# Six-block transformer kernel: a shorter opening, a branch laid the other way round, and new places for the pieces

## The reference

```python
x = x + xattn4(layernorm(x), ctx_1024, itok, ...)      # 4 layers, below, then rmsnorm
x = x + ternary_attention(layernorm(x), u, v)          # qz_u, qz_v, sigmoid, back through u and v
x = x + ffn(layernorm(x), weight, disha)
x = x + perceiver_attention(ctx_1024, layernorm(x), mask, ...)   # 64 latents over 1601+64 keys
x = x + rope_attention(layernorm(x), w_qkv, w_out)
x = x + experts(layernorm(x), ...)                     # 8 experts, the 2 best of a token

def xattn4(x, memory, seg_ids, ...):
    allowed = (j <= seg_ids) & (j > seg_ids - 128)      # j counts the rows of memory, seg_ids per token
    for l in range(4):
        h = rmsnorm(x, n1[l]); q, k, v = split(h @ Wqkv[l].T + bqkv[l])
        x = x + softmax(rope(q) @ rope(k).T * scale + causal) @ v @ Wo[l].T + bo[l]
        h = rmsnorm(x, n2[l]); kc, vc = split(memory @ Wkv_c[l].T)
        x = x + softmax((h @ Wq_c[l].T) @ kc.T * scale + cross_bias(allowed)) @ vc @ Wo_c[l].T
        h = rmsnorm(x, n3[l])
        x = x + silu(h @ Wg[l].T) * (h @ Wu[l].T) @ Wd[l].T
    return rmsnorm(x, nf)
```

## Time and profile before

| | |
|---|---|
| runs before | 500.36 us median, 498.7 to 501.63 |
| profiled execution | 499.64 us, span 497.5 us |
| PE busy | 465.2 us, 94% of the span |
| DVE, ACT, POOL busy | 358.0, 268.5, 227.9 us |
| opening, before the first matmul | 0 to 8.6 us |
| four layers | to about 215 us |
| the five other blocks | about 217 to 495 us |

### The profile page before, as it was taken

One profiled execution on the slowest core, in us unless ns is written; L12 is line 12 of the kernel. 1 busy time (PEld: TensorE's weight loads), 2 busy tenths in 40 slices (PEclk: granted clock), 3 DMA queues, 4 the chain that ended last, 5 costly groups with the idle time before them and its releaser, 6 DMA issues. The chain is left out here.

```text
span 497.5 us, 14297 instructions
## 1 busy us (share of the span) xinstructions
PE 465.2 (94%) x5430; PEld 401.7 (81%) x5430; DVE 358.0 (72%) x1025; ACT 268.5 (54%) x718; POOL 227.9 (46%) x342
## 2 busy tenths in 40 slices
PE   3899999999999999968999998899999998999997
PEld 3667887788778876967999887789999887689997
DVE  4395668566856786656887889999989987654643
ACT  4377757775777577614334475556466554442221
POOL 2871377137613851243799322767889322300000
PEclk9999999999999999979999999999999999999999
DMA  8601020101029000040210432031020000000000
GB/s 252 276 3 32 10 84 2 40 22 65 3 64 381 2 3 1 2 130 17 70 49 24 157 111 67 2 133 60 10 69 3 2 1 1 1 2 1 12 1 12
DMA packets 9953, 27.08 MB, mean 54 GB/s; under 512 B 1346, under 2 KB 4759, under 8 KB 9623
## 3 DMA queue, kind: packets, MB, share of 16 engines
q1 hardware_dynamic: 9878, 26.09, 15.5%
HBM read 25.82 MB, written 0.26 MB: 52 GB/s over the span
## 5 line engine op out<-in xcount | busy, mean ns | idle before, releaser
L913 POOL TENSOR_TENSOR rstd<-ss,par 128x1 f32<-128x1 f32 x52 | 28.5, 549 | 100.8 <-ACT sq L737 100.8
L759 ACT ACTIVATE pr<-sd 128x512 f32<-128x512 f32 x56 | 34.5, 626 | 5.4 <-DVE sd L816 4.9
L1243 POOL TENSOR_TENSOR xh<-xh,rsx 128x512 f32<-128x512 f32 (+1 forms) x32 | 29.8, 931 | 2.5
L1241 POOL TENSOR_TENSOR xh<-cx,mvx 128x512 f32<-128x512 f32 (+1 forms) x32 | 29.4, 918 | 2.7 <-DMA cx<-ctx_in 1.4
L741 ACT ACTIVATE h<-y,rstd 128x128 f32<-128x128 f32 x48 | 19.1, 399 | 9.5 <-POOL rstd L913 9.4
L1222 DVE BATCH_NORM_STATS2 stx<-cx 128x6 f32<-128x128 f32 x104 | 22.7, 276 | 0.5 <-DMA cx<-ctx_in 0.5
L1772 POOL TENSOR_TENSOR rstd<-mv,par 128x1 f32<-128x1 f32 x20 | 4.1, 207 | 39.8 <-DVE mv L1602 36.3
L737 ACT ACTIVATE sq<-y 128x129 f32<-128x129 f32 x52 | 15.9, 306 | 10.0 <-DVE y L847 8.6
L907 POOL TENSOR_TENSOR kblk<-qk,cf 128x512 f32<-128x512 f32 x20 | 20.8, 1040 | 0.9
L1232 POOL TENSOR_TENSOR rsx<-rsx,par 128x13 f32<-128x13 f32 x8 | 20.4, 2546 | 0.6
L1791 POOL TENSOR_SCALAR rk<-kss 128x8 f32<-128x8 f32 (+1 forms) x32 | 7.5, 235 | 24.0 <-DVE kss L1668 22.5
(11 more groups left out here) (570 smaller groups left out, 1507.2 us busy)
## 6 DMA issues: line engine op xcount, KB each, us to landing
cx<-ctx_in SPq DMA_DIRECT2D x13, 768.0 KB
we<-we_in SPq DMA_DIRECT2D x8, 514.0 KB, 7.1
wc<-wc_in SPq DMA_DIRECT2D x4, 768.5 KB, 5.8
wa<-wa_in SPq DMA_DIRECT2D x5, 387.0 KB, 3.0
wb<-wb_in SPq DMA_DIRECT2D x4, 256.5 KB, 3.8
uvT<-uvT_in SPq DMA_DIRECT2D x1, 1024.0 KB, 7.1
uv<-uv_in SPq DMA_DIRECT2D x1, 1024.0 KB, 8.6
cx<-ctx_in SPq DMA_DIRECT2D x13, 32.5 KB
```

The lines of the kernel that those rows point to most:

```text
L759: nc.scalar.activation(pr[:, t, at:at + 512], sd[:, t, at:at + 512], ACT.Exp).then_inc(s[piece], 1)
L913: nc.gpsimd.tensor_tensor(rstd[:, t:t + 1], ss[:, t:t + 1], par[:, 1:2], ALU.pow).then_inc(s[piece], 1)
L1241: step(pool, "pool_step", nc.gpsimd.tensor_tensor(part, cx[u % 2][:, tiles, :], mvx[:, b, tiles, 0].unsqueeze(2).to_broadcast(shape), ALU. ...
L1243: nc.gpsimd.tensor_tensor(part, part, rsx[:, b, tiles].unsqueeze(2).to_broadcast(shape), ALU.mult).then_inc(xm["c_normed"], 1)
```

## The change

1. SP issues `x` first, then one row of token values (`segi`, 1 partition) for the flag, then `cf`, `wa`, `bo`, `memT`, `wb`, `trig`, `cb`, and only then the broadcast `segr`.
2. DVE casts the one row into `pts`; `segf` and `cmask` come at the end of DVE's opening, behind `y`.
3. POOL zeroes `vblk` and `vcblk` at its very start; DVE copies `mem4` behind `y`. ACT's opening keeps only the two relus.
4. `FIRST` gives layer 0's `memory`, `mem_k`, `mem_v` and `kc` own places: no longer in front of everything but one by one between the pieces of the first half of layer 0. PE's queue now begins `turn1.0 project.0 turn1.1 values.0 project.1 memory.0 turn1.2 causal.0 values.1 project.2 scores.0 memory.1`, ACT's `square1.0 norm1.0 hT1.0 square1.1`, POOL's `pow1.0 pow1.1 pow1.2 rope_sum.0`.
5. The general path's semaphores share those of the CROSS pieces, and the 17 counts are made in the general path only.
6. On PE the branch is laid the other way round (`falls="end"`): the test is followed by the general path, and the fast one lies behind it, running straight on into `x_queue`.
7. ACT's and DVE's jump over their general path moves forward: on ACT before the last two `square_f`, on DVE before the last `z_moments`, `norm_f`, `x_f` and the last two `z_norm`. Those pieces are now in `x_queue`.
8. All places are given anew. In the layers this moves `memory`, `cmask`, `cturn`, `cout`, `turn3` and others by a few positions and POOL's `kc` ahead of `pow3`; behind the join some 20 positions differ on PE (`z_turn.2` now before `across0.0`), and POOL's `x_bias` comes later.

```diff
-PERIOD, SKEW = 95.43, (0.0, 6.74, 13.36, 19.85)
+PERIOD, SKEW = 95.05, (0.0, 6.68, 13.36, 19.84)
...
+FIRST = {"memory": 7.91, "mem_k": 8.44, "mem_v": 13.69, "kc": 9.26}
...
 def late(p, l, t):
-    return l * PERIOD + PLACE[p] + SKEW[t]
+    return l * PERIOD + (PLACE[p] if l else FIRST.get(p, PLACE[p])) + SKEW[t]
...
-        self.first = {e: 1 + max(n for n, z in enumerate(q) if z[1] == 0) for e, q in self.queue.items()}
+        self.first = {e: 1 + max(n for n, z in enumerate(q) if z[1] == 0 and not (e == "ACT" and z[2] == LAYERS) and
+                                 not (e == "DVE" and z[2] == LAYERS and z[3:] != (1, "z_norm"))) for e, q in self.queue.items()}
...
         def sp_opening(sp):
-            sp.dma_start(segr[:], seg_in.to_broadcast([P, B * L])).then_inc(s["seg_loaded"], 16)
             sp.dma_start(x[:], x_in.rearrange("(t p) d -> p t d", p=P)).then_inc(s["x_loaded"], 16)
+            sp.dma_start(segi[:], seg_in).then_inc(s["row_loaded"], 16)
+            sp.dma_start(cf[:], cf_in).then_inc(s["cf_loaded"], 16)
+            load_a(sp, 0)
             sp.dma_start(memT[:], memT_in).then_inc(s["mem_loaded"], 16)
             load_b(sp, 0)
-            sp.dma_start(cf[:], cf_in).then_inc(s["cf_loaded"], 16)
-            load_a(sp, 0)
             sp.dma_start(trig[:], trig_in).then_inc(s["trig_loaded"], 16)
             sp.dma_start(cb[:], cb_in).then_inc(s["trig_loaded"], 16)
+            sp.dma_start(segr[:], seg_in.to_broadcast([P, B * L])).then_inc(s["seg_loaded"], 16)
             sp.dma_start(nf[:], nf_in.to_broadcast([P, D])).then_inc(s["trig_loaded"], 16)
...
         def pool_opening(pool):
+            for blocks in (vblk, vcblk):
+                nc.gpsimd.memset(blocks[:], 0.0).then_inc(s["zeroed"], 1)
...
-            act.wait_ge(s["mem_loaded"], 16)
-            nc.scalar.copy(mem4[:], memT[:].unsqueeze(2).to_broadcast([P, B, 4, KF])).then_inc(s["zeroed"], 1)
-            for blocks in (vblk[:].rearrange("p t b j a e -> p (t b j a e)"), vcblk[:].rearrange("p b g i e -> p (b g i e)")):
-                nc.scalar.activation(blocks, par[:, 2:3].to_broadcast([P, B * 4 * 4 * 9]), ACT.Copy, scale=0.0).then_inc(s["zeroed"], 1)
...
-            for name in sorted(set(gsem) - {"ctx_loaded"}):
-                dve.sem_inc(gsem[name], 1)
             nc.vector.memset(y[:, :, D:D + 1], (RMS_EPS * D) ** 0.5).then_inc(s["y_ready"], 1)
-            dve.wait_ge(s["seg_loaded"], 16)
-            nc.vector.tensor_copy(segf[:], segr[:]).then_inc(s["seg_steps"], 1)
+            dve.wait_ge(s["zeroed"], 2)
...             (the ones into vblk and vcblk, moved here)
+            dve.wait_ge(s["row_loaded"], 16)
+            nc.vector.tensor_copy(pts[0:1, 0, 0:B * L], segi[:]).then_inc(s["seg_steps"], 1)
             dve.wait_ge(s["x_loaded"], 16)
...             (behind the four y)
+            dve.wait_ge(s["mem_loaded"], 16)
+            nc.vector.tensor_copy(mem4[:], memT[:].unsqueeze(2).to_broadcast([P, B, 4, KF])).then_inc(s["mem_spread"], 1)
+            dve.wait_ge(s["seg_loaded"], 16)
+            nc.vector.tensor_copy(segf[:], segr[:]).then_inc(s["cmask_set"], 1)
+            dve.wait_ge(s["cmask_set"], 1)
             dve.wait_ge(s["cf_loaded"], 16)
             nc.vector.tensor_scalar(cmask[:], segf[:], jcol, NEG, ALU.is_lt, ALU.mult).then_inc(s["cmask_set"], 1)
...
-        def either(eng, fast, whole):
+        def either(eng, fast, whole, falls="start"):
...
-            with eng.If(few == 1):
-                fast()
+            with eng.If(few == (1 if falls == "start" else 0)):
+                (fast if falls == "start" else whole)()
             with eng.Else():
-                whole()
+                (whole if falls == "start" else fast)()
...
-                either(pe, lambda: opening(pe, x_pe_piece, pe_piece, "PE"), whole)
+                either(pe, lambda: opening(pe, x_pe_piece, pe_piece, "PE"), whole, falls="end")
```

More of the change, by code:

```diff
@@ new lines @@
+    "PE": {"memory": -57.56, "turn1": -5.13, "project": 0.00, "values": 2.34, "causal": 8.35, "scores": 14.14,
+           "turna": 21.06, "turnb": 21.66, "weigha": 23.65, "weighb": 26.52, "turn_o": 27.96, "out": 30.78,
+           "turn2": 37.22, "qc": 38.13, "cmask": 40.25, "cscores": 40.99, "cturn": 48.74, "cweigh": 52.25,
+           "cturn_o": 54.41, "cout": 58.74, "turn3": 65.32, "gate": 67.23, "up": 71.70, "down": 79.16},
+    "ACT": {"square1": -11.89, "norm1": -8.90, "mem_k": -49.93, "hT1": -6.10, "q_groups": 9.94, "expa": 17.65,
+            "expb": 19.69, "turneda": 20.17, "turnedb": 22.51, "oT": 28.78, "square2": 31.68, "norm2": 33.63,
+            "hT2": 35.90, "qcT": 38.41, "cexp": 45.92, "cturned": 49.48, "coT": 54.02, "square3": 58.53,
+            "norm3": 59.59, "hT3": 63.65, "tanh": 67.72},
@@ L75 @@
+    "DVE": {"mem_v": -40.94, "rope": 2.09, "vblk": 7.76, "maxa": 15.75, "maxb": 15.97, "shifta": 16.67,
+            "shiftb": 17.90, "recip": 26.32, "o": 26.70, "y1": 31.71, "cmax": 42.03, "cshift": 43.26, "crecip": 52.40,
+            "co": 53.55, "y2": 58.61, "gated": 71.89, "hidden": 75.79, "y3": 80.30},
+    "POOL": {"pow1": -21.85, "rope_sum": -7.45, "rope_bias": -4.52, "k_groups": -3.52, "base": 3.86, "kc": -50.47,
+             "pow2": 17.57, "pow3": 51.67},
 }
 PLACE = {p: a for pieces in AT.values() for p, a in pieces.items()}
+FIRST = {"memory": 7.91, "mem_k": 8.44, "mem_v": 13.69, "kc": 9.26}
@@ L122 @@
 LAYER = {e: list(pieces) for e, pieces in AT.items()}
-FINAL = {"PE": {}, "ACT": {"square_f": 0.18}, "DVE": {"norm_f": 4.73, "x_f": 6.55, "z_moments": 10.88, "z_norm": 17.41},
-         "POOL": {"pow_f": -7.85, "z_power": 0.96}}
+FINAL = {"PE": {}, "ACT": {"square_f": -1.30}, "DVE": {"norm_f": 3.16, "x_f": 6.60, "z_moments": 9.27, "z_norm": 14.53},
+         "POOL": {"pow_f": -1.68, "z_power": 6.04}}
 for e in AT:
@@ L942, in queue @@
             for _, l, t, p in od.queue[engine]:
-                if within(p, l):
+                if within(p, l) and (l, t, p) not in JOINT.rest:
                     piece_of(eng, od, p, l, t)
@@ L1812, in x_queue @@
             fresh = False
-            for _, _, i, g, p in JOINT.queue[engine][JOINT.first[engine]:]:
+            for _, kind, i, g, p in JOINT.queue[engine][JOINT.first[engine]:]:
+                if kind == 0:
+                    layer_of(eng, FAST, p, i, g)
+                    continue
                 if p not in EARLY and not fresh:
@@ L1879, in whole @@
                 def whole():
+                    for name in sorted(set(gsem) - {"ctx_loaded"}):
+                        dve.sem_inc(gsem[name], 1)
                     dve.wait_ge(s["iota_loaded"], 32)
```

94 lines of the change are left out of this document (49 added, 45 removed).

## The result

The changed kernel is slower: 506.48 us against 499.39 us (medians of 15 runs each), ratio 1.0142, 95% interval 1.0119 to 1.0164. The ratios leave out a few executions of both kernels that ran long at a low clock, of the changed kernel one (513.36 us). The profiled execution has a span of 506.1 us against 497.5.

A forecast was written before the change was run, and what follows sets the result against it. PE's matmuls were taken to bound the layers, leaving gains at the opening and join: 0.75 + 1.5 = 2.3 us off the profiled 499.64 gives 497.3, median put at 497.5; range 493.8 to 501.2.

The forecast's parts named there:

- Loads, flag, zeros: Opening: earlier loads bring 0.5 us (y at 8.15, flag at 7.0); moved zeros and copies cost nothing.
- PE is then ready at 11.0: Opening: flag at 7.0, plus 1.1 for the branch and 2.9 for PE's jump, as measured at the join.
- Rival 3: Opening: PE's fetch at the branch waits for busy DMA engines; balance turns at 13.3, at 17 it is 503.3; chance 0.13.
- Each us after 11.0 is lost in full: Opening: if the fetch delays PE's start beyond 11.0 us, every further microsecond counts fully as loss.
- Layer 0: Start of layer 0: scores.0 at 20.7 against 23.45, 2.75 us earlier, before the owed memory pieces are subtracted.
- Minus three memory pieces, 2.0: Layer 0: three memory pieces still owed on a full PE at 0.67 us each, taking 2.0 off the 2.75.
- Opening gain: Opening and layer 0 together: 2.75 - 2.0 = 0.75 us won.
- 1.65 with PE's jump free: Upper end of the opening's gain, 1.65 us, if PE's jump at the flag costs nothing.
- New places in the layers: Layers: 0 taken; idle of 0.65 us a layer bounds the win to 2.6, and the loss to the same.
- The join: Join: PE running straight on gains 1.5 us, ends 0 and 3.4, with z_turn.2 waiting for z_norm.2 behind DVE's jump.
- 0 to 1.9, and I take 0.2: Behind the join: PE's 1.89 us "issue" pause before 229.80 may go, wholly or not; 0.2 us taken.
- The few swaps behind the join lie on a full PE: 0.: Behind the join: the few reordered pieces on a full PE change nothing, 0.

The follow-up runs named there:

- e9: e12 with one edit: PE's taken jump stands at the flag in the opening, as in the changed kernel, no longer at the join; 497.12 us, ratio 0.9966.
- e15: Changed kernel with the loads from layer 0's wc onward issued only when PE's first transpose is done; 505.11 us, ratio 1.0092.
- e16: e9 with the same edit as e15, loads held until PE's first transpose; 496.42 us, ratio 0.9929.
- e12: Changed kernel with the places of before in the layers and behind the join, and PE's branch as before; 498.02 us, ratio 0.9945.
- e3: Changed kernel with only PE's branch as before: straight on at the flag, jump at the join; 502.37 us, ratio 1.0051.
- e11: Changed kernel with the places behind the join of before and PE's branch as before; layers' places stay new; 502.16 us, ratio 1.0019.
- e14: e12 with the jumps of DVE and ACT at their places of before; 497.99 us, ratio 0.9961.
- e2: Changed kernel with the places behind the join of before (YWAY, YEACH, YAT, JOIN), the rest as changed; 501.90 us, ratio 1.0014.
- e13: Changed kernel with one swap in PE's queue put back: across0 of tile 0 ahead of z_turn.2; 502.37 us, ratio 1.0035.
- e17: Changed kernel with the swap of e13 and the bank choice of e10; 502.03 us, ratio 1.0031.
- e8: Changed kernel with the layers' places of before, everything else as changed; 499.00 us, ratio 0.9966.
- e1: Changed kernel with layer 0's memory pieces in front again (FIRST empty) and PE's branch as before; 505.85 us, ratio 1.0108.
- e4: Only the new opening (loads, flag, zeros, mem4 on DVE); memory pieces in front, places, jumps and branch as before; 499.54 us, ratio 0.9971.
- e10: Changed kernel with rope attention's first project (tile 0) forced into banks 0 and 1; 505.18 us, ratio 1.0105.

## Why the prediction was wrong

**Loads, flag, zeros.** Right in direction, too small: 1.15 us for the flag and 1.61 for `y` against 0.5 taken. `x`, issued at 0.74, landed 2.9 us later, at 3.6 and not at 5.1. The zeros were put at nothing because the row would land at 5; it landed earlier, so zeros and ones set the start of the cast (3.96), at about the time forecast for them (4.1). `segr` landed at 11.1 as said. Nothing of this gain reached PE.

**The branch in the opening: the step that failed first.** "PE is then ready at 11.0" took the quiet join's 2.9 us. Measured 7.1 us from the flag to the first `turn1`, 13.42. Rival 3 named the cause, put the point where gain turns to loss at 13.3 and gave it 0.13. e9, e15 and e16 show its size: 3.4 to 5.5 us from the flag until the packet moves, and 2.5 to 2.7 behind it, which is about the whole of the jump at the quiet join (2.56 in e12). "Each us after 11.0 is lost in full" was right up to `y1` (e3: 4.28 for 4.28). By the prediction's own sum this step turns a gain of 2.3 us into no change; the other 7 us of the result lie in the steps below.

**Layer 0.** "Minus three memory pieces, 2.0": four pieces come before the first `y1`, 3.5 us in e12, and two waits of 1.6 us together were not in the sum. Moved into the layer, the pieces change which bank each piece gets and who must have emptied it; in the changed kernel `project.3` waits 0.96 for shifts of earlier tiles. The queue was worked through, the banks were not. In the prediction's terms: `scores.0` is 0.75 us earlier than before (22.70) where 2.75 were forecast, and 3.6 are lost from there to `y1` where 2.0 were. Opening gain: 0.75 forecast, 2.9 lost, of which 2.4 is PE's later start. With PE's jump left at the join the gain at `y1` is 0.8 to 1.8 (e3, e11, e12, e14), and "1.65 with PE's jump free" looks right; that is luck in part: e12's `scores.0` comes 4.7 us earlier, not 3.65, and 3.5 of it are lost again, not 2.0.

**New places in the layers: "0".** 1.4 us lost in the profile over layers 1 to 3 (3.1 behind at the first `rope` of layer 1, 4.5 at the last `y3`), inside the bound of 2.6. e11 against e12 gives 0.7% in the medians, some 4 us, more than the two waits at L717 (1.2 us) explain.

**The join: 1.5.** `across0` started 2.0 us better against the layers' end than before, `z_turn.2` did wait for `z_norm.2` behind DVE's jump, and the high clock changed nothing, as said. But the sum stopped at `across0`. At `G` 0.8 is left; the pause in `M0` did not shrink but grew from 1.89 to 2.63. It was put at "0 to 1.9, and I take 0.2", with no cause. e2, e9, e13, e16 and e17 lose it and the changed kernel doesn't: its packet moves inside `M0`, theirs before it.

**"The few swaps behind the join lie on a full PE: 0."** The largest error. From `G` to the end the changed kernel loses 4.9 us in the profile, 2.7 of them between `x_added` and the first rope of block 5, at `project.0`'s bank. How much of the 4.9 is the order is not shown by the profile: its clock was at 0.50 for 10.2 us behind the join, which by itself could cost up to 5.1 us (an estimate: half of 10.2). The ratios, from ten and more runs each, do not hang on the clock of one execution: e2, which puts back the order at the join and behind it, puts the whole at 1.3% of the time, and e13 puts 1.1% on one swap. The bank alone they do not confirm (e17 against e13, and e8, which has the wait in full at 0.9966). A full PE says that a swap can't gain; it doesn't say that it can't lose.

**What stays open.** Why the swap of e13 is worth 5 us in the medians, of which its pause explains 2.6; why neither the two tables' costs nor the gains of e2 and e3 add; and why the clock fell behind the join in the profiles of the changed kernel, e1, e2, e3, e11, e13, e15 and e17, and before 490 us in none of the kernel before, e4, e8, e9, e12, e14 and e16. All of the first have the new layer places, but e10 has them too and kept its clock from 239 us on, so this may be chance.

## What to carry to other kernels

Before moving a taken jump to where the DMA engines are full, count 2.5 to 2.7 us behind its packet and the time until the packet moves (3.4 to 5.5 us here) as its price; and ask what the page after it will now collide with, since that decided whether the place that it left gave the price back (from the last `y3` to `G` 5.1 us, e9 against e12) or not (2.7, the changed kernel against e3). When pieces change places on a full engine, list the bank each one takes and who must have emptied it, for every piece that moves, before writing 0. Keep the parts of a change apart: here the new opening with the old places beats both kernels (e12 0.9945, e16 0.9929, against 1.0142 for the whole).

## What the runs showed of the hardware

The pause of 1.3 to 3.6 us inside a run of 128 matmuls of 64x64 goes with an instruction fetch. It falls behind the 49th of the second 64 (the 47th in e1), and ends 2.2 us behind an instruction packet in the changed kernel, 2.3 in e8 and 2.85 in the kernel before; where a packet moves 6 to 9 us sooner (222.0 in e13, 220.3 in e9, against 226.5 in e8 and 231.3), it is absent. What sets that moment is not shown. The Trainium skill ("Runtime: NRT & Kernel Launch", section "Instruction fetch mechanics") calls the crossing from one block of instructions to the next mostly hidden. Its block of 16 KiB agrees with the page (47 packets, 0.77 MB), but here the crossing is not hidden: the 128 matmuls take 2.1 us where nothing stops them (e9, 225.64 to 227.7), no more than the time from packet to work.

DVE's jump at the join cost 2.3 to 2.7 us (e17 2.26, e8 2.71), much as PE's there (e3 2.36, before 2.92).

A granted clock of 0.50 can lie over a wait at little cost: `across1` at 3.63 us with a wait of 0.82 in e8 takes 4.6 us from `z_turn.1` to `z_turn.2`, and `across1` at 2.02 with a wait of 2.15 in the changed kernel 4.3.
